# Three real products in place of four for the complex product of each bin, with the sums of the operands built on the other engines

## The reference, cut to what matters

```python
h = relu(_bn(_conv1d(xc, conv1_w, 0), ...))        # 1x1
h = _bn(_conv1d(h, conv2_w, 8), ...)               # 17 taps, 256 -> 256 channels
x_conv = transpose(relu(h + xc), (0, 2, 1))
```

## Time and profile before

| | us |
|---|---|
| median of 3 runs | 1857.56 (1856.35 to 1857.68) |
| the profiled execution | 1857.55 |
| its span in the profile | 1855.8 |
| PE busy | 1823.4, 98% of the span |
| DVE, ACT, POOL busy | 1170.7, 1027.6, 827.6 |
| filter units ahead of turn 0 | from 681.90 |
| turn 1 to the end of turn 39 on PE | 707.69 to 969.89 |

### The profile page before, as it was taken

The page is one execution under the profiler, slowest core; times in us unless marked ns, Lnnn a source line. Parts: engine busy times, 40 slices in busy tenths (PEclk is TensorE's granted clock), DMA queues, the critical chain, the costliest instruction groups (busy, mean ns, idle before and its releaser), DMA issues.

```text
span 1855.8 us, 29920 instructions
## 1 busy us (share of the span) xinstructions
PE 1823.4 (98%) x10268; PEld 1599.8 (86%) x10268; DVE 1170.7 (63%) x2251; ACT 1027.6 (55%) x1834; POOL 827.6 (45%) x1054
## 2 busy tenths in 40 slices
PE   5999999999999999999999999999999999999998
PEld 5999999999999998888888888888888888888886
DVE  8899998999888845444454454455455445445444
ACT  5998889898989865555553233233333323323322
POOL 6788888888777624333432122122122212212211
PEclk9999999999999999999999999999999999999999
DMA  6465656566555355655774544443443453454442
GB/s 200 138 215 187 207 192 207 188 208 213 186 186 196 130 161 132 156 140 139 170 223 116 119 83 101 115 92 94 114 103 86 110 120 78 102 119 83 101 108 40
DMA packets 513812, 262.56 MB, mean 141 GB/s; under 512 B 365575, under 2 KB 473479, under 8 KB 513662
## 3 DMA queue, kind: packets, MB, share of 16 engines
q1 hardware_dynamic: 512606, 260.52, 51.2%
q10 hardware_dynamic: 1056, 0.13, 0.0%
HBM read 151.51 MB, written 109.05 MB: 140 GB/s over the span
## 4 chain that ended last, share of the span: by engine, by line
PE 97%; DVE 1%; issue 0%; DMA 0%; ACT 0%; POOL 0%; SPq 0%; DVEq 0%; POOLq 0%; ACTq 0%
PE P L112 80%; PE P L892 5%; PE P L614 4%; PE P L662 4%; PE P L641 3%; PE P L633 1%; DMA col<-in_cols 0%; DMA yt<-y_d 0%; DVE hdxl L412 0%; PE P L1290 0%; DVE x L443 0%; DVE sm L491 0%; DVE sm L456 0%; POOL axl L544 0%; DVE wh0l L749 0%
## 5 line engine op out<-in xcount | busy, mean ns | idle before, releaser
L874 POOL TENSOR_TENSOR xnx1l<-xnf,xnx1h 128x1024 fp32r<-128x1024 f32 x16 | 44.3, 2771 | 346.2 <-ACT xnx1h L867 346.2
L874 POOL TENSOR_TENSOR xnx0l<-xnf,xnx0h 128x1024 fp32r<-128x1024 f32 x15 | 41.6, 2772 | 318.4 <-ACT xnx0h L867 318.4
L975 ACT ACTIVATE tr<-P,cold 128x512 f32<-128x512 f32 x64 | 44.2, 690 | 194.6 <-PE P L112 194.6
L978 ACT ACTIVATE nn<-gn,col 128x512 f32<-128x512 f32 x64 | 46.3, 724 | 179.3 <-DVE gn L992 179.3
L999 DVE SCALAR_TENSOR_TENSOR tz<-tz,tr 128x512 f32<-128x512 f32 x64 | 44.3, 692 | 148.0 <-ACT tz L982 148.0
L544 POOL TENSOR_TENSOR axl<-af,axh 128x512 fp32r<-128x512 f32 x64 | 91.9, 1435 | 101.7 <-ACT axh L370 101.7
L982 ACT ACTIVATE tz<-P,cold 128x512 f32<-128x512 f32 x64 | 44.1, 689 | 162.2 <-PE P L112 162.2
L988 DVE SCALAR_TENSOR_TENSOR gn<-tr,gn 128x512 f32<-128x512 f32 x64 | 44.2, 690 | 127.6 <-ACT tr L975 127.6
L112 PE MATMUL P<-w1mh,xxh 128*128 128x512 f32 x256 | 108.0, 422 | 0.0
L892 PEld LDWEIGHTS P<-gt,yt 128*128 128x128 f32 x768 | 98.8, 189 | 5.9 <-DMA yt<-y_d 1.0
L892 PE MATMUL P<-gt,yt 128*128 128x136 f32 (+1 forms) x768 | 101.2, 281 | 0.4 <-DMA yt<-y_d 0.3
(11 more groups left out here) (218 smaller groups left out, 6707.2 us busy)
## 6 DMA issues: line engine op xcount, KB each, us to landing
xh_d<-xst SPq DMA_DIRECT2D x64, 320.0 KB, 4.9
xl<-xh_d SPq DMA_DIRECT2D x40, 512.0 KB, 6.3
y_d<-yo SPq DMA_DIRECT2D x80, 256.0 KB, 2.4
x<-in_x SPq DMA_DIRECT2D x64, 256.0 KB, 3.0
a<-in_adj SPq DMA_DIRECT2D x64, 256.0 KB, 4.2
at<-in_adjt SPq DMA_DIRECT2D x64, 256.0 KB, 4.7
x_d<-x SPq DMA_DIRECT2D x64, 256.0 KB, 4.9
xn_d<-xt SPq DMA_DIRECT2D x64, 256.0 KB, 4.8
```

Source lines behind the costliest of these rows:

```text
L874: e.e.tensor_tensor(o[1][:, :, :], xnf[p % 2][:, :, :, :].rearrange("p c i t -> p c (i t)"), o[0][:, :, :], ALU.subtract).then_inc(done, 1)
L978: e.e.activation(nn[:, :], gn[:, :], ACT.Tanh, bias=n_b[:, o:o + 1]).then_inc(S["nn"], 1)
```

## The change

A bin's complex product is made of three real products of 256 output columns: (a+b)c, a(d-c) and b(-c-d). Row one is (a+b)c + b(-c-d), row two is (a+b)c + a(d-c). The filter's table gives d-c in place of d for the imaginary row, so that the second factor comes straight from the filter units; the third, -2c - (d-c), is made by DVE (`weights_sum`), and a+b by POOL (`spectra_sum`). Both sums are split into h and l like the other operands. The common product goes to a PSUM bank of its own, is copied to SBUF (`common_out`, half 0 on ACT, half 1 on DVE), and `freq_out`, now on DVE for both halves, adds it to the two others on the way out. All filter units are now moved off by ACT. `yo` has two buffers in place of four, `raw_wg` three in place of six, and some tiles lie elsewhere.

```diff
@@ tap_table
-        v = np.sin(2 * np.pi * k * f / NT) if im else np.cos(2 * np.pi * k * f / NT)
+        v = np.cos(2 * np.pi * k * f / NT)
+        if im:
+            v = np.sin(2 * np.pi * k * f / NT) - v
@@ tiles
...
+        xh = [p2.hl(f"xh{i}", [128, 3, 2, 256]) for i in range(3)]
+        wh = [p2.hl(f"wh{i}", [128, 3, 2, 256]) for i in range(2)]
+        xsum = p2("xsum", [128, 32, 16])
+        wsum = p2("wsum", [128, 2, 256])
+        mt = [p2(f"mt{i}", [128, 256]) for i in range(2)]
+        yo = [p2(f"yo{i}", [128, 512]) for i in range(2)]
@@ unit_out
-            if n % 2 == 0:
-                e.e.copy(dst, src).then_inc(S["wev0"], 1)
-            else:
-                e.e.tensor_copy(dst, src).then_inc(S["wev1"], 1)
+            e.e.copy(dst, src).then_inc(S["wev"], 1)
@@ spectra and weights
+        def spectra_sum(e, f):
+            e.wait_ge(S[f"lxh{f // 2 % 2}"], 2 * loaded(f // 2, 2))
+            e.wait_ge(S["xslo"], f - 1)
+            e.wait_ge(S["xshi"], f - 1)
+            x = bin_of(f)
+            e.e.tensor_tensor(xsum[:, :, :], x[:, 0], x[:, 1], ALU.add).then_inc(S["xsum"], 1)
 
         def spectra_hi(e, f):
             e.wait_ge(S[f"lxh{f // 2 % 2}"], 2 * loaded(f // 2, 2))
             e.wait_ge(S["frq"], 2 * f - 4)
-            for c in range(2):
-                t = e.e.copy(by_group(xh[f % 3][0], c), bin_of(f, c))
-            t.then_inc(S["xhi"], 1)
+            e.e.copy(parts_of(xh[f % 3][0]), bin_of(f)).then_inc(S["xhi"], 1)
+            if f:
+                e.wait_ge(S["xsum"], f)
+                e.e.copy(sum_of(xh[f % 3][0]), xsum[:, :, :]).then_inc(S["xshi"], 1)
 
         def spectra_lo(e, f):
+            h, l = xh[f % 3]
             e.wait_ge(S["xhi"], f + 1)
             e.wait_ge(S["frq"], 2 * f - 4)
-            for c in range(2):
-                t = e.e.tensor_tensor(by_group(xh[f % 3][1], c), bin_of(f, c), by_group(xh[f % 3][0], c), ALU.subtract)
-            t.then_inc(S["xlo"], 1)
+            e.e.tensor_tensor(parts_of(l), bin_of(f), parts_of(h), ALU.subtract).then_inc(S["xlo"], 1)
+            if f:
+                e.wait_ge(S["xshi"], f)
+                e.wait_ge(S["xsum"], f)
+                e.e.tensor_tensor(sum_of(l), xsum[:, :, :], sum_of(h), ALU.subtract).then_inc(S["xslo"], 1)
...
+        def weights_sum(e, f):
+            e.wait_ge(S["wev"], UNITS * (f // 10 + 1))
+            e.wait_ge(S["wslo"], f - 1)
+            e.wait_ge(S["wshi"], f - 1)
+            w = weights_of(f)
+            e.e.scalar_tensor_tensor(out=wsum[:, :, :], in0=w[:, 0, :, :], scalar=-2.0, in1=w[:, 1, :, :],
+                                     op0=ALU.mult, op1=ALU.subtract).then_inc(S["wsum"], 1)
 
         def weights_hi(e, f):
...
-            e.e.copy(both(wh[f % 2][0]), weights_of(f)).then_inc(S["whi"], 1)
-            e.e.mul(wh[f % 2][0][:, :, 0, :], weights_of(f)[:, 1, :, :], -1.0).then_inc(S["wnhi"], 1)
+            e.e.copy(wh[f % 2][0][:, 0:2, :, :], weights_of(f)).then_inc(S["whi"], 1)
+            if f:
+                e.wait_ge(S["wsum"], f)
+                e.e.copy(wh[f % 2][0][:, 2, :, :], wsum[:, :, :]).then_inc(S["wshi"], 1)
 
         def weights_lo(e, f):
...
-            e.e.tensor_tensor(both(l), weights_of(f), both(h), ALU.subtract).then_inc(S["wlo"], 1)
-            e.wait_ge(S["wlo"], f + 1)
-            e.e.tensor_scalar(l[:, :, 0, :], l[:, :, 2, :], -1.0, None, ALU.mult).then_inc(S["wneg"], 1)
+            e.e.tensor_tensor(l[:, 0:2, :, :], weights_of(f), h[:, 0:2, :, :], ALU.subtract).then_inc(S["wlo"], 1)
+            if f:
+                e.wait_ge(S["wshi"], f)
+                e.wait_ge(S["wsum"], f)
+                e.e.tensor_tensor(l[:, 2, :, :], wsum[:, :, :], h[:, 2, :, :], ALU.subtract).then_inc(S["wslo"], 1)
@@ freq (f > 0)
-            e.wait_ge(S[f"ye{chunk}"], f - 1)
+            e.wait_ge(S["ye"], n - 1)
+            e.wait_ge(S[f"mt{chunk}"], f - 1)
...
-                for c in range(2):
-                    for q in range(2):
-                        t = multiply(e.e, mm3([{0: x_(h, c, q)} for h in range(2)],
-                                              [{0: w[:, c, 1 - q:3 - q, :].rearrange("p q o -> p (q o)")} for w in wb],
-                                              o[:, :], c == 0 and q == 0, c == 1 and q == 1, [(0, 0)]))
+            e.wait_ge(S["xshi"], f)
+            e.wait_ge(S["xslo"], f)
+            product(common(chunk)[:, 0:256], 2, 0).then_inc(S["com"], 1)
+            product(main(chunk)[:, 256:512], 0, 1)
+            e.wait_ge(S["wshi"], f)
+            e.wait_ge(S["wslo"], f)
+            product(main(chunk)[:, 0:256], 1, 2).then_inc(S["frq"], 1)
+
+        def common_out(e, f, chunk):
+            n = 2 * f + chunk
+            e.wait_ge(S["com"], n - 1)
+            e.wait_ge(S["ye"], n - 1)
+            if chunk == 0:
+                e.e.copy(mt[0][:, :], common(0)[:, 0:256]).then_inc(S["mt0"], 1)
+            else:
+                e.e.tensor_copy(mt[1][:, :], common(1)[:, 0:256]).then_inc(S["mt1"], 1)
@@ freq_out
...
+            e.wait_ge(S[f"sy{chunk}"], 16 * f)
+            if f == 0:
+                e.e.tensor_copy(yo[chunk][:, :], main(chunk)[:, :]).then_inc(S["ye"], 1)
+                return
+            e.wait_ge(S[f"mt{chunk}"], f)
+            e.e.tensor_tensor(yo[chunk][:, :].rearrange("p (q o) -> p q o", q=2),
+                              main(chunk)[:, :].rearrange("p (q o) -> p q o", q=2),
+                              mt[chunk][:, :].unsqueeze(1).broadcast_to((128, 2, 256)),
+                              ALU.add).then_inc(S["ye"], 1)
@@ load_wg
+            e.wait_ge(S["wg"], c - 2)
@@ ACT's loop over f
                 if f + 1 < NF:
                     weights_hi(e, f + 1)
+                if f:
+                    common_out(e, f, 0)
                 if f + 2 < NF:
                     spectra_hi(e, f + 2)
                 for n in units_in(f, 0):
-                    if n % 2 == 0:
-                        unit_out(e, n)
-                freq_out(e, f, 0)
+                    unit_out(e, n)
                 for n in units_in(f, 1):
-                    if n % 2 == 0:
-                        unit_out(e, n)
+                    unit_out(e, n)
@@ DVE's loop over f
                 if f + 1 < NF:
+                    weights_sum(e, f + 1)
                     weights_lo(e, f + 1)
-                for n in units_in(f, 0):
-                    if n % 2:
-                        unit_out(e, n)
-                for n in units_in(f, 1):
-                    if n % 2:
-                        unit_out(e, n)
+                freq_out(e, f, 0)
+                if f:
+                    common_out(e, f, 1)
                 freq_out(e, f, 1)
                 if gates_at(f) is not None:
                     split_wg_lo(e, gates_at(f))
@@ POOL's loop over f
             for f in range(NF):
+                if f:
+                    spectra_sum(e, f)
                 spectra_lo(e, f)
```

More of the change, by code:

```diff
@@ L155, in gnn_kernel @@
         cold = keep("cold", [128, 24])
-        ft = keep("ft", [128, 2 * NT])
         gt = keep("gt", [128, 416])
@@ L168, in gnn_kernel @@
         wf = [keep("wf0", [128, 20, 2, 256])]
-        raw_wg = [third(f"st_wg{c}", [128, 768]) for c in range(6)]
+        raw_wg = [third(f"st_wg{c}", [128, 768]) for c in range(3)]
         xnf = [third(f"xnf{i}", [128, 2, 2, 256]) for i in range(2)]
         nms = [third(f"nms{i}", [128, 2, 256]) for i in range(2)]
-        yt = [third(f"yt{i}", [128, 3, 256]) for i in range(2)]
+        yt = [third(f"yt{i}", [128, 3, 256]) for i in range(3)]
+        xnx = [third.hl("xnx0", [128, 2, 512])]
         p1, p2, p3 = Place(nc, keep.at), Place(nc, keep.at), Place(nc, keep.at)
+        ft = p1("ft", [128, 2 * NT])
         hdx = p1.hl("hdx", [128, 2, 256])
@@ L671, in unit_out @@
             e.wait_ge(S["unit"], n + 1)
-            e.wait_ge(S["wnhi"], 10 * (part - 1))
+            e.wait_ge(S["whi"], 10 * (part - 1))
             e.wait_ge(S["wlo"], 10 * (part - 1))
@@ L758, in freq, with product @@
             e.wait_ge(S["whi"], f + 1)
-            e.wait_ge(S["wneg"], f + 1)
-            e.wait_ge(S["wnhi"], f + 1)
-            e.wait_ge(S[f"ye{chunk}"], f - 1)
+            e.wait_ge(S["wlo"], f + 1)
+            e.wait_ge(S["ye"], n - 1)
+            e.wait_ge(S[f"mt{chunk}"], f - 1)
             xb, wb = xh[f % 3], wh[f % 2]
-            def x_(h, c, q):
-                return xb[h][:, c, q, 128 * chunk:128 * chunk + 128]
+            def product(o, q, k):
+                return multiply(e.e, mm3([{c: x[:, q, c, 128 * chunk:128 * chunk + 128] for c in range(2)} for x in xb],
+                                         [{c: w[:, k, c, :] for c in range(2)} for w in wb],
+                                         o, True, True, [(0, 0), (1, 1)]))
@@ L779, in freq @@
-            t.then_inc(S["frq"], 1)
+                product(main(chunk)[:, 0:256], 0, 0)
+                product(main(chunk)[:, 256:512], 1, 1).then_inc(S["frq"], 1)
```

(11 more changed lines are left out.)

72 lines of the change are left out of this document (26 added, 46 removed).

## The result

| | before | after |
|---|---|---|
| median of six runs each, us | 1856.45 (1856.12 to 1857.68) | 1864.45 (1863.11 to 1868.27) |
| the profiled execution, us | 1857.55 | 1863.11 |
| its span | 1855.8 | 1861.2 |
| first filter unit on PE | 681.90 | 679.25 |
| turn 1 | 707.69 | 707.77 |

The ratio is 1.0046, with an interval of 1.0033 to 1.0059: the change costs about 8 us. It is slower, as forecast, by less than the 11.8 us forecast. (The forecast's 1869.4 is counted from the median of the first three runs, 1857.56; counted from the 1856.45 here it would be 1868.3.)

What follows compares the result with a forecast made beforehand. PE bounds the kernel before; after, the path DVE and POOL share does. 710.5 + 38 x 6.89 + 5.0 = 977.3, plus turn 39's 4.4, ends at 981.7, 11.8 us later: 1869.4 us, range 1852 to 1891.

Steps and rivals of the forecast that it cites:

- The bound: Stage of the bins: the path DVE and POOL share sets the turn at 6.89 us, above PE's 6.6 and 4.4.
- the signs: Stage of the bins: PE about 65% busy in turns 29 to 38, turns about 6.9, 7.7 in 32 to 37.
- The holds: Each turn: POOL needs the shared path for 4.53 us and DVE for 2.21, 6.74 together.
- bare start: Once a turn POOL starts with nobody queued in front, its start-up uncovered: 0.15 us, giving 6.89 a turn.
- Rival 3: Shared path: whole instructions of DVE and POOL exclude each other, 38 x 0.65 us more, 1894; chance 0.06.
- Rival 2: Shared path: partial overlap, holds a tenth shorter, 6.4 us a turn, 1851; chance 0.10.
- rival 1: Stage of the bins: the shared path is no bound, PE stays it, faster, 1822 us; chance 0.08.
- `split_wg_lo`: Six turns: DVE's 768-element subtraction holds the shared path for 0.83 us (0.56 to 1.09), 5.0 us in all.
- rival 4: DVE's and POOL's lists leave the shared path empty when ACT's high part comes late: 7.8 us a turn, 1904; chance 0.09.
- The start: Start of the bins' stage: turn 1 starts at 710.5 in place of 707.69, 2.8 us later (1.2 to 4).
- The last turn: Turn 39 on PE, without filter units: 4.4 us, ending at 981.7.
- rival 5: PE in eleven turns: clock falls to 1.2 GHz, 36 matmuls take 8.6 us, 1.8 more each, 1890; chance 0.03.

Runs made afterwards that it cites:

- four late products: The changed kernel with the four-product matmuls of the kernel before in turns 30 to 39, three products in turns 1 to 29: 1849.27 us, ratio 0.9961.
- both edits: The changed kernel with four products in turns 30 to 39 and the weights' sum in PSUM in turns 1 to 29: 1836.27 us, ratio 0.989.

## Why the prediction was right, and where its sizes were off

**The bound.** PE's turn would be 4.4 without units and the path's above it: turn 39 took 4.38, the regular others 6.71. Right, and shown by runs that differ in the place of one operand: an addition with one input in PSUM costs the regular turns nothing, with both in SBUF it lengthens them; the rest of `weights_sum` taken off the path shortens the turns without units from 6.71 to the 6.18 of the sum of holds. (That last run also takes one of four PSUM banks from the filter units.) PE's turn with units was put a little high: 6.45 with three units is 4.32 + 3 x 0.72, and no run shows the 0.2 for changes of kind. Of the signs, turns 32 to 37 have the mean of 7.7 that was forecast, but run from 6.2 to 9.7, and PE is busy for 71% in turns 29 to 38 in place of 65%, at a granted clock of 0.86.

**The holds.** 6.74 was forecast without the bare start, and 6.71 came. Rival 3, whole instructions excluding each other, would give 7.54 a turn and falls. The same for the rule of the Trainium skill (SBUF — State Buffer, Who interferes with whom) that the pair is held for the whole instruction: every line of the round above ends one hold, and not one whole instruction, behind the other engine's. Two sentences of the same section of the Trainium skill agree with the runs: one SBUF input does not contend (0.43 and 0.685, undisturbed), two do. Rival 2, holds a tenth shorter, falls by the same 6.71, and rival 1 with it. (A tenth off the holds is 6.1, or 6.2 with the bare start; how the prediction came to 6.4 it does not say.)

**The bare start of 0.15 a turn** is the term that was mis-sized, and the largest error. I held that once a turn POOL starts with nobody in front. In the round, POOL's 1024 starts at 808.13 and waits under DVE's rest until 808.73: nobody ever starts bare, since each engine's next operation is already waiting when the other ends. That is 38 x (6.89 - 6.71) = 6.8 us too much. The run with the semaphore in POOL's list shows the start when it is bare: 0.15 from the 2.39, and 0.08 for the hand-over, 0.21 to 0.23 a turn. So 0.15 was about the right size for something that does not happen in this round.

**`split_wg_lo`:** 5.0 forecast by its hold, 46.07 - 6 x 6.71 = 5.8 in the profile, 6.3 between medians. The size is right, the mechanism isn't quite. Two turns take nearly all of it. It shifts DVE's list by one hold, and in turn 33 DVE's rest arrives after POOL has begun, DVE and then POOL:

```profile
924.54 1.39 DVE L893 TENSOR_TENSOR wgl<-st_wg,wgh 128x768 fp32r<-128x768 f32 x1
925.85 1.78 DVE L755 SCALAR_TENSOR_TENSOR wsum<-wf 128x512 f32<-128x512 f32 x1
927.56 2.30 DVE L770 TENSOR_TENSOR wh0l<-wf,wh0h 128x1024 fp32r<-128x1024 f32 x1
929.78 2.82 DVE L774 TENSOR_TENSOR wh0l<-wsum,wh0h 128x512 fp32r<-128x512 f32 x1
```

```profile
929.58 2.47 POOL L741 TENSOR_TENSOR xh2l<-xl,xh2h 128x1024 fp32r<-128x1024 f32 x1 [0.81 <-ACT xh2h L732]
...
938.51 2.42 POOL L741 TENSOR_TENSOR xh0l<-xl,xh0h 128x1024 fp32r<-128x1024 f32 x1 [3.37 <-ACT xh0h L732]
```

POOL starts 0.20 ahead of DVE's line 774, which takes 2.82 for work of 0.68, and PE's next bin waits for it. Then POOL waits 3.37 for ACT's high part, and in that time DVE runs alone. So rival 4 happens, in turns 33 and 35 and not in all. Turn 1 is 8.04 for a related reason: POOL's 1024 starts at 707.88, 0.05 ahead of `weights_sum`, which takes 2.90. There the path never gets empty. From the end of DVE's rest at 706.81 to the next at 714.74 it is held seven times in place of six, with `spectra_sum` twice.

**The start:** 2.8 forecast, 2.73 measured. **The last turn:** 4.4 and 4.38. **The first stage** and **what lies behind the stage** were put at nothing: the first was 2.65 shorter here, which is a matter of the execution, the second 0.74 longer. With turn 1's 1.33, the 0.8 of `split_wg_lo` and 0.2 in small ones, these terms lead from the 981.7 forecast for the first gate product to the 974.55 seen: -2.65 - 6.8 + 1.33 + 0.8 + 0.2 = -7.1.

**PE's clock, rival 5.** I wrote that nothing shows it. It falls, but in the change it was nearly all hidden. Stretches of turns 29, 30, 34 and 36 (the number behind POOL's is the granted clock; the last two reach 0.2 into the next turn):

```profile
897.16:903.90 6.74, 4.58 (x37) 4.41 (x37) 6.61 (x7) 4.48 (x7) 6.66 (x4) 0.99 0.84 208
903.90:910.60 6.70, 6.00 (x37) 5.82 (x37) 6.57 (x7) 3.19 (x5) 6.56 (x4) 0.76 0.59 166
```

```profile
933.67:940.07 6.40, 6.40 (x38) 6.40 (x39) 5.56 (x7) 3.09 (x5) 2.89 (x3) 0.67 0.46 162
949.50:956.45 6.95, 6.95 (x38) 6.95 (x39) 5.67 (x7) 3.09 (x5) 3.44 (x3) 0.61 0.53 191
```

The matmuls of turn 30 and of turn 34, from PE's timeline:

```profile
903.86 0.55 PE L114 MATMUL P<-wh0h,xh0h 128*128 128x256 f32 x1 [2.15 <-ACT wh1h L761]
...
933.67 0.55 PE L114 MATMUL P<-wh0h,xh1h 128*128 128x256 f32 x1 [5.18 <-DVE yo L829]
934.02 0.42 PE L114 MATMUL P<-wh0l,xh1h 128*128 128x256 f32 x1
934.24 0.41 PE L114 MATMUL P<-wh0h,xh1l 128*128 128x256 f32 x1
```

After a rest of 2.15 and one of 5.18 the matmuls come 0.21 apart, which is 0.12 at the other level: 1.2 in place of 2.4 GHz. In turn 30 some fifteen of the 36 run so, in turn 36 more than twenty. A turn of 36 matmuls is then 6.0 to 6.8 us long on PE, against 6.7 of the path. The loss fits into the rest that caused it: turn 30 is 6.68, like the others. Only in turn 36 (6.77 long, with PE busy throughout, and DVE idle for 1.04 until PE is done) PE may have set the time. In turn 10, which has units and comes behind a rest of 2.14, the slow matmuls don't fit in:

```profile
769.48:776.77 7.29, 7.29 (x49) 7.29 (x49) 6.96 (x7) 2.92 (x5) 7.15 (x4) 0.77 0.31 97
```

PE is busy throughout and the turn is 7.29, but turns 11 and 12 make it good with 6.45 each. The rule of the Trainium skill that the prediction cited (TensorE: Matmul & The Clock Gate, HAM oscillation) agrees with these rows in kind; rival 5's price, 1.8 us in each of eleven turns, isn't paid, since at 8.6 a turn it took all 36 matmuls for slow, and 0.24 for each in place of the 0.21 seen. With four products in these turns the clock is 1.00.

**What stays open.** Turns 2 to 8 take either 6.71 or about 8.0, in patterns that differ from kernel to kernel: turns 2, 3, 5 and 6 take 7.95, 7.79, 8.03 and 8.01 with four late products, and 6.71 to 6.73 in the change; with both edits turns 3 and 4 take 7.58 and 8.00, and the semaphore in POOL's list didn't alter that. The stretches of these two turns:

```profile
721.47:729.05 7.58, 5.52 (x48) 5.34 (x46) 5.11 (x7) 5.07 (x10) 7.50 (x5) 1.00 0.95 208
729.05:737.05 8.00, 8.00 (x55) 8.00 (x55) 6.62 (x7) 4.90 (x10) 7.86 (x4) 0.79 0.27 100
```

In the first PE rests for 2.06 at full clock. In the second it is busy throughout at 0.79 and sets the length itself, with DVE idle for 1.01 behind it. So with units in the turn the lower clock is paid for: 8.00 in place of 6.45. The same pair, a turn of 7.6 to 8.0 at 1.00 and then one of 7.95 to 8.02 at 0.79 with PE busy throughout, stands in the kernels with four late products (turns 1 and 2, 5 and 6), with the sum in PSUM (3 and 4) and with the addition from PSUM (1 and 2, 5 and 6). What starts the first turn of a pair wasn't tested.

## What to carry to other kernels

Before work is moved to DVE and POOL, add up the holds of what they share, DVE's operations with two SBUF inputs and all of POOL's, by turn: here two engines that were half idle got 3.4 us of it more in each turn, which made it 6.74, above PE's 4.4 in the turns without units and slightly above its 6.45 in the others. An operand in PSUM takes an operation off that path, here at the price of one of the filter units' four banks: it turned a loss of 8 us into a gain of 8, and using the sums only in the turns where PE has other work besides gave a kernel 20 to 21 us (1.1 to 1.2%) faster than the one before. Taking work off an engine pays only in the turns where that engine is the bound.

## What the runs showed of the hardware that was not expected

- DVE and POOL alternate over the shared path in the order in which they come, without a gap, as long as both have the next one waiting: in a round of six operations each ends one hold behind the other's (1.14, 1.08, 1.15, 0.55, 2.24, 0.56), and the start of each lies under the other. A semaphore between them lays it bare, for 0.21 a turn (2.47 from end to end in place of 2.24).
- Who comes 0.20 too late waits for the whole of the other's hold: 2.82 us for an operation of 0.68. So a small extra operation can cost more than its own hold: +21.5 us for 39 operations of 256 elements with a hold of 0.28 each, though the lower clock of PE has a part in that.
- PE's granted clock falls with rests of only 2.15 us, and in every other turn: 0.99, 0.76, 1.00 and 0.74 in turns 29 to 32. A slow turn shortens the rest behind it (0.70 ahead of turn 31), and the turn after runs at full clock. Without filter units the loss fits into the rest; with them a turn of 6.45 became 8.00 at 0.79.
